# An FFT-gated convolution block: buffer starts at 64 bytes, a transposition group inside a matmul chunk, two PSUM copies on VectorE

## The reference

```
x = x + L0(gn(x));  x = x + L1(gn(x))
L0: out = conv1_w @ depthwise3x3(x * sigmoid(pooled), sum_k softmax(att)_k * weight_k) + conv1_b
L1: hidden = depthwise3x3(w_hidden @ x, w_dw);  q, k, v = split(hidden, 3)      # 64 channels each
    out  = irfft2(rfft2(patches8x8(q)) * rfft2(patches8x8(k)))
    out  = layernorm over the 64 channels of each pixel (norm_w, norm_b)
    return w_out @ (v * out)
```

## Time and profile before

| | |
|---|---|
| median of three runs | 2349.22 us (2339.35 to 2354.64) |
| the profiled execution's own time | 2354.21 us |
| its span, first to last instruction | 2352.2 us |
| TensorE matmul busy | 2192.9 us, 93% |
| VectorE busy | 1869.5 us, 79% |
| ScalarE busy | 1527.0 us, 65% |
| GpSimd busy | 501.7 us, 21% |
| mean granted TensorE clock | 0.973 |

### The profile page before, as it was taken

One profiled execution on the slowest core, in us unless ns is written; L12 is line 12 of the kernel. 1 busy time (PEld: TensorE's weight loads), 2 busy tenths in 40 slices (PEclk: granted clock), 3 DMA queues, 4 the chain that ended last, 5 costly groups with the idle time before them and its releaser, 6 DMA issues.

```text
span 2352.2 us, 99348 instructions
## 1 busy us (share of the span) xinstructions
PE 2192.9 (93%) x44279; PEld 1343.9 (57%) x44279; DVE 1869.5 (79%) x4570; ACT 1527.0 (65%) x2629; POOL 501.7 (21%) x323
## 2 busy tenths in 40 slices
PE   6888888868999999999999999999999999999997
PEld 3333333335666666666666666666666666666663
DVE  4667656646888888888888888888888888888886
ACT  4556555566766767666666667777667667676662
POOL 1000000001222222222222222222222222222222
PEclk9989888888999999999999999999999999999998
DMA  7789888885333333333333333333333333333312
GB/s 139 179 212 236 222 200 217 210 196 118 75 76 76 76 75 76 76 76 80 80 80 80 80 81 89 70 87 85 80 81 76 85 76 76 76 76 76 76 43 51
DMA packets 60381, 248.08 MB, mean 105 GB/s; under 512 B 12393, under 2 KB 12658, under 8 KB 53810
## 3 DMA queue, kind: packets, MB, share of 16 engines
q1 hardware_dynamic: 59954, 241.72, 43.7%
HBM read 139.96 MB, written 101.72 MB: 103 GB/s over the span
## 4 chain that ended last, share of the span: by engine, by line
PE 75%; DVE 14%; issue 5%; ACT 4%; DMA 1%; POOL 0%; SPq 0%; ACTq 0%; POOLq 0%
PE bank L526 16%; PE bank L586 15%; PE bank L657 10%; PE bank L645 9%; PE bank L608 6%; PE bank L674 6%; PE bank L571 6%; PE bank L599 5%; DVE arena L1108 5%; DVE arena L1204 2%; DVE arena L1128 2%; DVE arena L1121 2%; ACT arena L861 2%; DVE arena L1098 1%; ACT arena L816 1%
## 5 line engine op out<-in xcount | busy, mean ns | idle before, releaser
L455 POOL TENSOR_TENSOR arena<-arena 128x8 f32<-128x8 f32 x256 | 477.5, 1865 | 1330.2 <-DVE arena L1114 1330.0
L586 PE MATMUL bank<-arena 128*64 128x512 f16 x4608 | 710.2, 395 | 3.9 <-DVE arena L1133 0.2
L807 ACT ACTIVATE arena<-bank 100x512 f32<-100x512 f32 x1024 | 692.4, 761 | 26.5 <-PE bank L571 23.8
L571 PEld LDWEIGHTS bank<-arena 128*36 128x36 f16 (+1 forms) x8192 | 324.1, 104 | 255.7 <-ACT arena L807 32.7
L526 PE MATMUL bank<-arena 32*32 32x508 f32 (+1 forms) x9216 | 384.4, 648 | 54.1 <-issue 39.4
L571 PE MATMUL bank<-arena 128*36 128x128 f16 (+1 forms) x8192 | 405.6, 221 | 19.0 <-DVE arena L1098 11.5
L1204 DVE TENSOR_TENSOR arena<-bank,arena 128x512 f32<-128x512 f32 x512 | 329.0, 684 | 77.2 <-issue 76.5
L816 ACT ACTIVATE arena<-bank,arena 128x256 f32<-128x256 f32 x512 | 260.4, 560 | 127.4 <-PE bank L599 127.4
L849 ACT ACTIVATE arena<-bank 128x512 f32<-128x512 f32 x256 | 153.0, 598 | 271.6 <-PE bank L645 271.0
L1108 DVE BATCH_NORM_STATS2 arena<-arena 128x6 f32<-128x128 f32 x1024 | 265.5, 322 | 37.3 <-ACT arena L861 37.3
L657 PE MATMUL bank<-arena 100*32 100x128 f32 x8192 | 278.1, 274 | 3.7 <-issue 3.6
(11 more groups left out here) (114 smaller groups left out, 1739.0 us busy)
## 6 DMA issues: line engine op xcount, KB each, us to landing
arena<-xn_d SPq DMA_DIRECT2D x128, 536.2 KB, 4.8
xn_d<-arena SPq DMA_DIRECT2D x130, 260.0 KB, 4.5
x_d<-arena SPq DMA_DIRECT2D x64, 512.0 KB, 7.8
arena<-x_d SPq DMA_DIRECT2D x128, 256.0 KB, 4.2
out<-arena SPq DMA_DIRECT2D x128, 256.0 KB, 2.7
arena<-x_in SPq DMA_DIRECT2D x32, 544.0 KB, 9.9
arena<-x_in SPq DMA_DIRECT2D x32, 528.0 KB, 9.5
arena<-spectra_in SPq DMA_DIRECT2D x1, 384.0 KB
```

What stands on the lines that cost most here:

```text
L455: pool.tensor_tensor(tiny["rstd"][:, slot], tiny["var_eps"][:, slot], powers, ALU.pow).then_inc(s_root, 1)
L571: mm = pe.matmul(ring[g % len(ring)][low:high, 128 * i:128 * i + 128], w[:, first + low:first + high], hidden_w, start=True, stop=True)
L586: mm = pe.matmul(v_banks[chunk % 3][64 * s:64 * s + 64, :], v_w[:, 64 * tap:64 * tap + 64], at(xs[u % 3], row * WP + 32 * k + dx, [32 * WP ...
L807: act.activation(h_rows[0:WIN, :, first:first + 4], ring[g % len(ring)][0:WIN, :].rearrange("p (i c) -> p c i", i=4), ACT.Copy).then_inc(s ...
```

## The change

take rounds the start of every buffer of 16 words or more up to a multiple of 16 words (64 bytes). All the buffers named above then start at 0 modulo 64, so that a pair of floats in Y that began 12 bytes into a piece of 16 bytes now begins at 0, and one that began at 4 now begins at 8.

The four copies of inverse(3) are shared out: ScalarE keeps banks 0 and 1, VectorE takes banks 2 and 3 behind its three windows and raises a new semaphore y_last. The counts of y_ready change from 16 to 14 a unit.

turn(tail, 0, 0) is no longer between two chunks but behind the third tap of v_chunk(tail, 1, 0). In VectorE's order window 3 comes after scale(0) and no longer ahead of centre(0).

```diff
+            if words >= 16:
+                top[0] = -(-top[0] // 16) * 16
...
-                if g < 3 and positive(16 * u):
-                    pe.wait_ge(s_y_ready, 16 * u - 3 + g)
+                if g < 2 and positive(14 * u):
+                    pe.wait_ge(s_y_ready, 14 * u - 1 + g)
+                if g == 2 and positive(2 * u):
+                    pe.wait_ge(s_y_last, 2 * u - 1)
...
+                    if tap == 2 and middle is not None:
+                        middle()
...
-                    turn(tail, k, 0)
+                    if k > 0:
+                        turn(tail, k, 0)
                     if k < 3:
-                        v_chunk(tail, k + 1, 0, (5, 4, 3)[k], hidden)
+                        v_chunk(tail, k + 1, 0, (5, 4, 3)[k], hidden, None if k > 0 else lambda: turn(tail, 0, 0))
...
-                for c in range(4):
+                for c in range(4 if e < 3 else 2):
...
+            def last_inverse_out(u):
+
+                dve.wait_ge(s_inverse_mm, 4 * u + 4)
+                for c in (2, 3):
+                    dve.tensor_copy(Y_out[:, 48 + c:64:4, :, :],
+                                    i_banks(3)[c][:, 256:512].rearrange("p (c s j) -> p c s j", s=2, j=32)).then_inc(s_y_last, 1)
...
                 if p == 0:
-                    dve.wait_ge(s_y_ready, 16 * (u + 1))
+                    dve.wait_ge(s_y_ready, 14 * (u + 1))
+                    dve.wait_ge(s_y_last, 2 * (u + 1))
...
                 variance(tail, 0)
-                windows()
                 centre(tail, 0)
                 pixel_stats(tail, 1)
                 variance(tail, 1)
                 scale(tail, 0)
+                windows()
...
                     for r in range(3):
                         window(u + 1, r)
+                last_inverse_out(u)
```

More of the change, by code:

```diff
@@ L186, in build @@
         s_y_ready = semaphore("y_ready")
+        s_y_last = semaphore("y_last")
         s_pixel_stats = semaphore("pixel_stats")
@@ L279, in build @@
         prod = take(4 * 1024)
-        assert top[0] <= first_image_free
+        assert top[0] <= first_image_free, (top[0], first_image_free)
         Y = take(64 * 64)
@@ L573, in hidden_group, with v_chunk @@
                 mm.then_inc(s_hidden_mm, 1)
-            def v_chunk(u, k, jr, groups, between):
+            def v_chunk(u, k, jr, groups, between, middle=None):
                 chunk = 2 * k + jr
                 if chunk < 3:
-                    pe.wait_ge(s_y_ready, 16 * u + 9 + chunk)
+                    pe.wait_ge(s_y_ready, 14 * u + 9 + chunk)
                 else:
@@ L664, in inverse @@
                     if 0 < e < 3:
-                        pe.wait_ge(s_y_ready, 16 * u + 4 * e)
+                        pe.wait_ge(s_y_ready, 14 * u + 4 * e)
                     if e == 0 and tail is not None:
@@ L1089, in _ @@
             Y4 = Y.rearrange("p (s c j) -> p s c j", s=2, j=32)
+            Y_out = Y.rearrange("p (s c j) -> p c s j", s=2, j=32)
             over = lambda a: a.rearrange("p (s j) -> p s j", s=2).unsqueeze(2).broadcast_to([128, 2, 64, 4])
```

## The result

The changed kernel takes 2314.77 us, the median of four runs (2311.2 to 2316.74), against 2348.36 us before (four runs, 2339.35 to 2354.64). The ratio is 0.9858, with a 95% interval of 0.9828 to 0.9887: 33.6 us or 1.4% faster. The forecast was 2311. Its profiled execution took 2316.74 us, with a span of 2314.7.

The account below looks back on a forecast made before the run. TensorE was taken to set the pace, held three times a front by one VectorE chain; 31 fronts gave 36.6 us and the last 2, together 38.6, hence 2311 us, range 2302 to 2320.

Parts of the forecast that it names:

- Term 1: Front, VectorE: with two of inverse(3)'s copies moved to it, the statistics start 0.36 us earlier, 0.20 without any overlap.
- Term 2: VectorE on Y: rounded starts take 0.18 us a piece off bn_stats and 0.04 us each off centre and scale.
- Term 3: Front: scale(0), waiting for GpSimd's root, starts 0.56 us earlier; 0.81 earlier if the root takes 1.90 us.
- Term 4: VectorE, scale(0) to gate(0): window 3 comes in, the stretch takes 4.82 us, and gate(0) starts 0.54 us earlier.
- Term 5: TensorE: fourth chunk gains gate(0)'s 0.54 us, project(0) stops waiting for gate(1) and gives 0.64: 1.18 us a front.
- the starts bring nothing: Rival: rounded starts do not shorten bn_stats, gate(0) comes 0.12 us later than before; 2352 us, chance 0.15.
- the starts help TensorE: Rival: the matmuls of q and k also get faster from rounded starts, 17 us more; 2294 us, chance 0.12.
- The third: Rival: VectorE's PSUM copies take 0.68 us each and the starts bring nothing, gate(0) 0.8 us later; 2374 us, chance 0.05.

Follow-up runs that it names:

- The swapped pairs: The kernel before with the two bn_stats of each pair in the other order; 2352.02 us in one run, period 55.99 us.
- the displaced Y: The changed kernel with all starts rounded but that of Y, 12 bytes past a multiple of 64; 2342.02 us, ratio 0.9988.
- all four kernels of the first table: The kernel before, the changed kernel (2314.77 us), the kernel before with only the rounded starts (2307.18 us), the changed kernel without them (2349.49 us).
- hwin displaced: The changed kernel with all starts rounded but that of hwin, 12 bytes past a multiple of 64; 2316.78 us, ratio 0.9883.

## Why the prediction was right, and where it was not

**Term 1** (the statistics 0.36 us earlier): 0.31. The pair of copies took 0.75 us from the start of the first to the end of the second, against 0.76 assumed, and the first started 0.08 ahead of the windows' end, as assumed; but the statistics started 0.10 behind the second's end and not 0.05.

**Term 2** (0.09 us off the first and third bn_stats, 0.04 off centre and scale): 0.368 became 0.281, and centre and scale lost 0.045 and 0.051. The swapped pairs and the displaced Y show the cause, and that all eight pieces pay before shows that the boundary is one of 16 bytes.

**Term 3** (scale(0) 0.56 us earlier, with a root of 2.15): 0.51, with a root of 2.15. With the starts alone, where window 3 is still between the variance and centre(0), it takes 1.90, and with the copies on ScalarE and centre(0) next to it, 2.15. So what runs on VectorE when the root starts makes the 0.25 us. The prediction named the Trainium skill (SBUF — State Buffer, section SBUF: two separate sides) for this, by which a VectorE operation with two SBUF inputs and a GpSimd operation that reads SBUF lock each other out. The trace agrees: the root takes 2.15 us where centre runs at its start, and 1.64 where gate does, whose second input is in PSUM. The shorter root is most of why the starts alone reach scale(0) at 5.68, 0.10 behind the changed kernel, though their statistics start 0.30 later.

**Term 4** (gate(0) 0.54 us earlier): 0.42. The stretch from scale(0) to gate(0) took 4.90 us for 4.82, since the instruction behind scale(0), centre(1) and scale(1) started 0.61 to 0.63 us behind them before and 0.60 to 0.61 after: the three give 0.06 us and not 0.12. scale(0) itself was 0.05 less early than forecast (term 3), which makes the rest.

**Term 5, the step that failed**, is the one on project(0). The prediction said that its second matmul starts "half of 1.02 later" and that nothing is left to wait for. The two matmuls write the two halves of the bank's partitions and run side by side: each is two instructions in the records, and undisturbed, in project(1) of one front before, the four start at 0.00, 0.00, 0.43 and 0.43 us, with the next transposes 0.96 us behind the start of project. In all four kernels of the first table the third transposes start 1.06 us behind gate(1)'s end. So the second matmul, which needs gate(1), takes about as long as the whole, and must start with the first if nothing is to be lost. gate(1) ended 0.28 us behind project(0)'s start in the changed kernel, where it should have ended 0.27 behind by the forecast too (1031.47 against 1031.20). So the wait gave back 0.25 us and not 0.64, and the front gained what gate(1) gained, 0.67, and by the next inverse 0.74 us, not 1.18. With that corrected the prediction's own gate(1), 0.80 us earlier, would have given 25 us for the fronts instead of 36.6. The 0.07 us between 0.67 and 0.74 lie behind the third transposes: from there to the next inverse it is 39.55 us before, 39.48 with all starts rounded and 39.51 with Y or hwin displaced.

The same term had TensorE wrong ahead of the fourth chunk too, which changed nothing in the sum. It put the third chunk at 1022.61, 5.71 us behind the inverse; it started at 5.09, since the faster drains into hwin, which the prediction did not price, no longer held up the hidden groups (5.54 with hwin displaced). So the transposes still wait 0.15 us for scale(0), and the wait ahead of the fourth chunk is 0.95 us and not 0.75. gate(0) sets the chunk either way.

**The sum.** 38.6 us were forecast, and the medians differ by 33.6. But between the two profiled executions, which differ by 37.5, only 26.0 us are in the places of the forecast (24.3 in the fronts, 1.7 in the last, for 36.6 and 2). 4.0 us came ahead of the first unit's inverse(3), which was put at nothing, and 7.4 in the first stage, which scatters by more than that. So the range held and the chain of VectorE was the one named, but the fronts and the last unit alone fall short of the lower bound of 29 us: that 2314.8 lies in the range, and so near 2311, is partly luck.

**The rivals.** That the starts bring nothing is refuted by the kernel with them alone; but what the rival said would happen to the moves without them, 2352 us and the wait in its new place, did happen when they were run alone (2349.49). That the starts help TensorE is refuted as well, 274 and 275 ns. The third needed copies of 0.68 us each; they take 0.42.

## What to carry to other kernels

When an engine waits, follow the chain of the engine that it waits for to the next place where the same chain is needed, before moving the waiting work: the same transposes moved out of a wait of 1.06 us were worth 0.00, and 0.18 us once the chain had been shortened. Where VectorE or ScalarE reads or writes many runs of 8 or 16 bytes, look at the start of the buffer modulo 16; two lines in an allocator were worth more here without the three moves than with them. And put work that nobody waits for (the windows) behind the instruction that is waited for, even where both fit.

## What the runs showed of the hardware

- VectorE reading 64 pairs of floats: 0.28 us where no pair straddles a 16-byte boundary, 0.37 where each does, so about 1.4 ns for each. All eight pieces paid in the kernel before, where only two would cross a multiple of 64 and four one of 32, so the boundary is one of 16. Adding 16 to all starts changed nothing.
- ScalarE writing 128 runs of 16 bytes a partition, out of PSUM: 604 to 615 ns, and 749 to 761 where each straddles, 1.1 to 1.2 ns a run by 607. It held up TensorE's hidden groups, and VectorE's chain hid that here.
- VectorE with centre and scale (128 runs of 16 bytes read and written): 0.045 to 0.051 us more where each straddles, about 0.4 ns a run, much less than for the pairs.
- GpSimd's power over 128x8 goes by what VectorE is in when it starts: 1.64 us for gate, 1.90 for a window copy, 2.02 to 2.15 for scale, 2.15 to 2.18 for centre, and 2.24 for centre with a window copy starting later beside it. In the last four it is longer than 1.64 by what VectorE's instruction still has to run, less about 0.15 us (0.41 us left give 1.90, 0.66 give 2.15), but for the 0.09 of the later window; gate with 0.52 us left adds nothing. A centre and a scale that start behind the root do not lengthen it. Two roots of the front in the earlier trace rows of the kernel before, the first 0.16 us behind the start of scale(0), the second 0.16 us behind that of gate(0), with centre and scale in its time as well:

```profile
1023.16 2.02 POOL L455 TENSOR_TENSOR arena<-arena 128x8 f32<-128x8 f32 x1 [0.45 <-DVE arena L1114]
...
1027.96 1.64 POOL L455 TENSOR_TENSOR arena<-arena 128x8 f32<-128x8 f32 x1 [0.32 <-DVE arena L1114]
```
